# Attention scored in eighths of a unit: own and relative scores mixed on TensorE's row groups, with a block of sums behind each eighth

## The reference

```
q, k, v = conv1x1(wq, xn), conv1x1(wk, xn), conv1x1(wv, xn)     # n, head, c, i, j
qk  = einsum('nhcij,nhciw->nhijw', q, k) / D                    # own scores, a 128 x 128 matrix for each row i
qrq = einsum('nhcij,chjw->nhijw', q, rq) / D                    # relative scores, for each column j
krk = einsum('nhcij,chjw->nhijw', k, rk) / D
weight = softmax(qk + Gq * qrq + Gk * krk, axis=3)              # over j
out = einsum('nhijw,nhciw->nhcij', weight, Gv1 * v)             # v sums, for each i
    + einsum('nhijw,chjw->nhcij', weight, Gv2 * rv)             # r sums, for each j
x = x + conv1x1(wo, out)
```

## Time and profile before

| | us |
|---|---|
| median of 3 runs | 8287.58 |
| lowest and highest | 8284.58, 8298.17 |
| the profiled execution | 8291.75 |
| span of its trace | 8290.0 |
| TensorE busy | 7187.2 (87%) |
| VectorE busy | 5176.6 (62%) |
| ScalarE busy | 4856.3 (59%) |
| GpSimd busy | 2457.0 (30%) |

### The profile page before, as it was taken

One profiled execution on the slowest core, in us unless ns is written; L12 is line 12 of the kernel. 1 busy time (PEld: TensorE's weight loads), 2 busy tenths in 40 slices (PEclk: granted clock), 3 DMA queues, 4 the chain that ended last, 5 costly groups with the idle time before them and its releaser, 6 DMA issues. The chain is left out here.

```text
span 8290.0 us, 275612 instructions
## 1 busy us (share of the span) xinstructions
PE 7187.2 (87%) x106442; PEld 6044.4 (73%) x106442; DVE 5176.6 (62%) x20646; ACT 4856.3 (59%) x11427; POOL 2457.0 (30%) x1235
## 2 busy tenths in 40 slices
PE   4999999799999999999999899999999966766738
PEld 3555555689988888898899898898888932332338
DVE  5444444366666666666666666666666768988830
ACT  1444444577777777777777777777777733333410
POOL 0000000243443443444434444434434432322210
PEclk7999999666666666666666666666667688988855
DMA  7555555565655665655556656656656576766522
GB/s 217 203 203 204 204 204 197 113 112 100 112 103 98 113 107 101 107 99 107 101 106 112 102 100 109 109 99 110 105 100 109 92 232 203 265 201 202 208 74 99
DMA packets 1721071, 1148.11 MB, mean 138 GB/s; under 512 B 1143009, under 2 KB 1506145, under 8 KB 1703329
## 3 DMA queue, kind: packets, MB, share of 16 engines
q1 hardware_dynamic: 1530336, 842.56, 48.1%
q10 hardware_dynamic: 188352, 285.27, 9.3%
q0 software_dynamic: 1024, 2.09, 0.1%
HBM read 708.04 MB, written 421.56 MB: 136 GB/s over the span
## 5 line engine op out<-in xcount | busy, mean ns | idle before, releaser
L787 POOL TENSOR_TENSOR att_scores<-att_scores,att_inverse 128x1024 f32<-128x1024 f32 x1024 | 1966.8, 1934 | 2951.7 <-DVE att_inverse L722 2951.7
L660 ACT ACTIVATE att_scores<-att_scores,att_negmax 128x128 f32<-128x128 f32 x8192 | 2509.2, 399 | 67.6 <-issue 67.6
L737 DVE CUSTOM_DVE_ANT_0 att_scores<-att_ps,att_scores 128x128 f32<-128x128 f32 x8192 | 1780.8, 286 | 1066.7 <-PE att_ps L573 957.5
L560 PE MATMUL att_ps<-att_qk,att_rs 32*128 32x64 f32 x32768 | 1793.2, 380 | 155.6 <-ACT att_scores L652 114.2
L560 PEld LDWEIGHTS att_ps<-att_qk,att_rs 32*128 32x128 f32 x32768 | 1698.6, 299 | 196.2 <-ACT att_scores L652 142.5
L573 PE MATMUL att_ps<-att_own 16*128 16x128 f32 x16384 | 1541.6, 405 | 231.3 <-issue 224.1
L573 PEld LDWEIGHTS att_ps<-att_own 16*128 16x128 f32 x16384 | 1416.2, 300 | 268.9 <-issue 264.4
L652 ACT ACTIVATE att_scores<-att_ps 128x1024 f32<-128x1024 f32 x1024 | 992.4, 1021 | 1044.3 <-PE att_ps L560 1044.3
L720 DVE TENSOR_REDUCE att_total<-att_scores 128x8 f32<-128x1024 f32 x1024 | 1233.7, 1205 | 70.7 <-issue 70.7
L594 PE MATMUL att_ps<-att_scores,att_rv 128*16 128x64 f32 x32768 | 1249.6, 334 | 11.0 <-issue 10.8
L594 PEld LDWEIGHTS att_ps<-att_scores,att_rv 128*16 128x16 f32 x32768 | 1193.6, 127 | 24.5 <-issue 13.1
(11 more groups left out here) (146 smaller groups left out, 5276.0 us busy)
## 6 DMA issues: line engine op xcount, KB each, us to landing
qk<-proj_qk_out ACTq DMA_DIRECT2D x64, 2048.0 KB, 8.5
att_qk<-qk SPq DMA_DIRECT2D x512, 256.0 KB, 6.7
att_own<-qk SPq DMA_DIRECT2D x2048, 64.0 KB, 2.5
proj_x<-in_x_dram SPq DMA_DIRECT2D x128, 512.0 KB, 4.3
v_t<-proj_v_out ACTq DMA_DIRECT2D x64, 1024.0 KB, 11.3
att_vt<-v_t SPq DMA_DIRECT2D x128, 512.0 KB, 5.5
att_v<-att_att_v SPq DMA_DIRECT2D x512, 128.0 KB, 4.2
att_r<-att_att_r SPq DMA_DIRECT2D x512, 128.0 KB, 3.5
```

The source lines that it names most:

```text
L560: last = pe.matmul(ps[:, 4 + g, jj * IU:(jj + 1) * IU], rs[32 * g:32 * g + 32, t * JB + jj, :], qk[b][32 * g:32 * g + 32, :, t * JB + jj], ...
L660: last = act.activation(scores[v][:, i, :], scores[v][:, i, :], ACT.Exp, bias=negmax[v][:, i:i + 1], scale=-1.0)
L737: last = dve.tensor_tensor_reduce(out=scores[v][:, i, :], in0=ps[:, 2 * (p % 2) + r // 4, (r % 4) * W:(r % 4 + 1) * W], in1=scores[v][:, i ...
L787: pool.tensor_tensor(scores[v][:, rows, :], scores[v][:, rows, :], inverse[v][:, rows].unsqueeze(2).broadcast_to([P, PR, W]), ALU.mult).th ...
```

## The change

Own and relative scores are computed together, in eighths of a unit. `ROUNDS` goes from 4 to 8: a relative round now uses two row groups, 2 * (1 - t % 2) and the next, and banks 4 and 5. `scores_of` issues own piece p of unit u on two row groups, and between its matmuls those of a relative round on the other two: round p+2 of unit u+1 for p under 6, round p-6 of unit u+2 for p of 6 and 7. Own operands are 32 rows, of which the upper 16 are zeroed once (`cleared`). After each eighth PE does half of a v fill in bank 6 (8 matmuls) and half of an r fill in bank 7 (16 matmuls): fills 2 and 3 of unit u-2 in the first four eighths, fills 0 and 1 of unit u-1 in the others.

ACT reads a relative round with one instruction, issues exps with a counter per four rows, and reads an r fill behind every second eighth. DVE reads all four v fills and sums rows two pieces behind. `att_v`, `att_r` and `vt` are two halves each; att_r is stored in DRAM in 8 pieces (`STORES_R`), the combine phase reads them so. SP issues the stores of unit u-2 in two parts (16 DMAs a unit in place of 8), the v values in two, `rv` in four; the qk load stands ahead of the first stores. POOL's two scalings of the relative tables stand ahead of pieces 3 and 7 of the seventh unit, before ahead of 2 and 4. Two calls of `unit` stand behind the last unit in place of one.

```diff
-ROUNDS = JG // JB
+ROUNDS = 2 * JG // JB
+HR = PR // 2
+HALVES = IU // HR
-JT = JG
+JT = JG // 2
+STORES_G = JG // JT
...
             def unit(h, k, u, started, left):
                 if started >= 1:
                     sp.wait_ge(own_done, PIECES * u)
                     load_own(h, k, 1)
-                if started >= 2:
-                    store(*before(h, k, 2), u - 2)
-                if started >= 1:
-                    ph, pk = before(h, k, 1)
-                    later(sp, v_done, FILLS * (u - 1))
-                    load_v(ph, pk)
-                    if pk == 0:
-                        later(sp, r_done, FILLS * (u - 1))
-                        load_rv(ph)
                 if left >= 2:
                     sp.wait_ge(rel_done, ROUNDS * u + ROUNDS)
                     load_qk(*after(h, k, 2))
+                if started >= 2:
+                    store(*before(h, k, 2), u - 2, 0)
+                if started >= 1:
+                    ph, pk = before(h, k, 1)
+                    later(sp, v_done, FILLS * (u - 2) + FILLS // 2)
+                    load_v(ph, pk, 0)
...
                 if left >= 1:
                     sp.wait_ge(own_done, PIECES * u + PIECES // 2)
                     load_own(*after(h, k, 1), 0)
+                if started >= 1:
+                    later(sp, v_done, FILLS * (u - 1))
+                    load_v(ph, pk, 1)
...
+                if started >= 2:
+                    store(*before(h, k, 2), u - 2, 1)
...
+            def relative(u, v, t, jj, gg):
+                g, j = 2 * (1 - t % 2) + gg, t // 2 * JB + jj
+                return pe.matmul(ps[:, 4 + gg, jj * IU:(jj + 1) * IU], rs[32 * g:32 * g + 32, j, :], qk[v % 2][32 * g:32 * g + 32, :, j],
+                                 start=True, stop=True, tile_position=(32 * g, 0))
+            def own_score(u, p, r, gg):
+                half, g, at = p // (PIECES // 2), 2 * (p % 2) + gg, p % (PIECES // 2) // 2 * 4 + r
+                return pe.matmul(ps[:, g, r * W:(r + 1) * W], own[half][32 * g:32 * g + 32, 1, at, :], own[half][32 * g:32 * g + 32, 0, at, :],
+                                 start=True, stop=True, tile_position=(32 * g, 0))
+            def scores_of(u, p, now, ru, rv_, t, rel_on):
...
                 for r in range(4):
                     for gg in range(2):
+                        if now:
+                            last_own = own_score(u, p, r, gg)
+                        if rel_on:
+                            for x in range(2):
+                                last_rel = relative(ru, rv_, t, 2 * r + gg, x)
...
+            def unit(u, v, parts):
+                back2, back1, now, ahead1, ahead2 = parts
+                for p in range(PIECES):
+                    if p < 6:
+                        scores_of(u, p, now, u + 1, v + 1, p + 2, ahead1)
                     else:
+                        scores_of(u, p, now, u + 2, v + 2, p - 6, ahead2)
+                    if p < 4 and back2:
+                        sums_with_v(u - 2, v - 2, 2 + p // 2, p % 2)
+                        sums_with_r(u - 2, v - 2, 2 + p // 2, p % 2)
+                    if p >= 4 and back1:
+                        sums_with_v(u - 1, v - 1, p // 2 - 2, p % 2)
+                        sums_with_r(u - 1, v - 1, p // 2 - 2, p % 2)
...
+            def read_relative(u, o, t):
+                pair = 2 * (1 - t % 2)
...
+                act.activation(scores[o % BUFS][:, :, :].rearrange("w i (g j) -> w i g j", g=G)[:, :, pair:pair + 2, t // 2 * JB:(t // 2 + 1) * JB],
+                               ps[:, 4:6, :].rearrange("w g (j i) -> w i g j", i=IU), ACT.Copy).then_inc(rel_read, 1)
...
+            def unit(u, v, parts):
+                for p in range(PIECES):
+                    if p == 0:
+                        if back1:
+                            exp_half(u - 1, v - 1, HALVES - 2)
+                            exp_half(u - 1, v - 1, HALVES - 1)
+                    elif now:
+                        exp_half(u, v, 2 * p - 2)
+                        exp_half(u, v, 2 * p - 1)
+                    if p < 6 and ahead1:
+                        read_relative(u + 1, v + 1, p + 2)
+                    if p >= 6 and ahead2:
+                        read_relative(u + 2, v + 2, p - 6)
+                    if p % 2 and p < 4 and back2:
+                        read_r(u - 2, 2 + p // 2)
+                    if p % 2 and p >= 4 and back1:
+                        read_r(u - 1, p // 2 - 2)
...
-                        if k == UPH - 2 and not last and p in (2, 4):
-                            scale_relative(h + 1, p // 2 - 1)
+                        if k == UPH - 2 and not last and p == 3:
+                            scale_relative(h + 1, 0)
+                        if k == UPH - 2 and not last and p == 7:
+                            scale_relative(h + 1, 1)
```

More of the change, by code:

```diff
@@ L529, in _ @@
                 load_qk(0, k)
+            sp.wait_ge(cleared, 2)
             for half in range(2):
@@ L556, in relative @@
                 if t % (ROUNDS // 2) == 0:
                     pe.wait_ge(rs_ready[t // (ROUNDS // 2)], u // UPH + 1)
[L558 to L565 removed]
+                later(pe, rel_read, ROUNDS * u + t)
@@ L593, in sums_with_r @@
+            def sums_with_r(u, v, b, half):
+                if half == 0:
+                    pe.wait_ge(rv_loaded[b], (u // UPH) * 16 + 16)
+                    later(pe, r_read, FILLS * u + b)
+                for jj in range(half * JB // 2, (half + 1) * JB // 2):
                     for g in range(G):
-                        last = pe.matmul(ps[32 * g:32 * g + HD, bank, jj * IU:(jj + 1) * IU], rv[:, g * JG + b * JB + jj, :], scores[v][:, :, g * JG + b * JB + jj],
+                        j = g * JG + b * JB + jj
+                        last = pe.matmul(ps[32 * g:32 * g + HD, 7, jj * IU:(jj + 1) * IU], rv[:, j, :], scores[v % BUFS][:, :, j],
@@ L640, in _ @@
+            pe.wait_ge(cleared, 3)
             for t in range(ROUNDS):
-                relative(0, 0, t)
+                scores_of(0, 0, False, 0, 0, t, True)
+            for t in range(2):
+                scores_of(0, 0, False, 1, 1, t, True)
             units(pe, unit)
@@ new lines, in read_relative, with exp_half @@
+                act.activation(scores[o % BUFS][:, :, :].rearrange("w i (g j) -> w i g j", g=G)[:, :, pair:pair + 2, t // 2 * JB:(t // 2 + 1) * JB],
+                               ps[:, 4:6, :].rearrange("w g (j i) -> w i g j", i=IU), ACT.Copy).then_inc(rel_read, 1)
+            def exp_half(u, v, p):
+                act.wait_ge(added, HALVES * u + p + 1)
+                for r in range(HR):
+                    i = p * HR + r
+                    last = act.activation(scores[v % BUFS][:, i, :], scores[v % BUFS][:, i, :], ACT.Exp, bias=negmax[v % BUFS][:, i:i + 1], scale=-1.0)
+                last.then_inc(exped, 1)
@@ L710, in _ @@
             for t in range(ROUNDS):
                 read_relative(0, 0, t)
+            for t in range(2):
+                read_relative(1, 1, t)
             units(act, unit)
@@ L741, in unit @@
[L741 to L771 removed]
+                    if r % HR == HR - 1:
+                        last.then_inc(added, 1)
@@ new lines, in _, with unit @@
+            BEHIND = 2
+            def unit(u, v, parts):
+                back2, back1, now, ahead1, ahead2 = parts
+                for p in range(PIECES):
+                    if now:
+                        add_and_largest(u, v, p)
+                    if p % 2 == 1 and p < 4 and back2:
+                        read_v(u - 2, 2 + p // 2)
+                    if p % 2 == 1 and p >= 4 and back1:
+                        read_v(u - 1, p // 2 - 2)
+                    k = p - BEHIND
+                    if k >= 0 and now:
+                        sums_of(u, v, k)
+                    elif k < 0 and back1:
+                        sums_of(u - 1, (v - 1) % BUFS, PIECES + k)
@@ L773, in _ @@
+            for half in range(2):
+                dve.memset(own[half][:, :, :, :], 0.0).then_inc(cleared, 1)
+            dve.memset(ps[:, 6:8, :], 0.0).then_inc(cleared, 1)
             units(dve, unit)
```

286 lines of the change are left out of this document (88 added, 198 removed).

## The result

The changed kernel takes 7861.41 us (7833.53 to 7865.77, four runs), the kernel before 8286.08 in the same comparison: a ratio of 0.9478, with a 95% interval of 0.9454 to 0.9502. Its profiled execution took 7833.53 us, with a span of 7831.8.

A forecast was written before the change was run, and what follows sets the result against it. Attention was taken as bound by TensorE, mostly at half clock. Unit 32.6 + 3.75 + 2.1 = 38.45 against 40.05 us, times 124, -198; prologue +36, combine +5: 8291.75 becomes 8135 profiled, 8130 forecast, range 7880 to 8900.

The forecast's parts named there:

- blocks of 2 us would not win the clock back: Attention, after a pause: short sums may regain full clock late; 1.2 units per head taken at half clock.
- An eighth on PE alone: PE in attention: scores, v sums, r sums and turns of one eighth take 3.81 us at full clock.
- The tables: Next head's relative tables, loaded by SP and scaled by POOL: PE waits 12 us per head where it waited 4.
- The prologue: Before attention: four relative rounds of 5.75 us become ten of about 4.8, +27 us.
- Combine: Combine stage, bound by DVE: r sums are read in pieces half as long, +5 us, bounds 0 and 20.
- The loop's pauses: PE at and just behind the turn of the loop over four units: pauses stay, 18 us per head.
- ACT's chain: ACT's exps, relative reads and r read: a pair of eighths takes 8.15 us, an undisturbed unit 32.6.
- The v values: SP's loads for the v sums: named among those queued behind a late store, with no separate price.
- The rival that rested on this queue: SP's issues fill the unit: 9 to 12 us more per head, 8270 to 8320 us, chance 0.12.
- The clock's price: Attention: 1.2 units per head at half clock, 13.8 us each, add 2.1 us per unit.
- the "better" case: Row groups overlap more, or rounds ahead cover pauses: unit 35 to 36.9 us, total 7700 to 7940, chance 0.10.
- The turn between tile modes: PE between sums and scores: 0.2 us a turn, 2 turns a unit become 16, +2.8 us.

The follow-up runs named there:

- the block experiments: Changed kernel with a unit's sums gathered into one, two or four blocks in place of eight: 9711.82, 9612.95 and 8935.01 us.
- p_pad40: Kernel before, with 40 already met waits on PE ahead of its first relative round, shifting its later instructions: 8160.04 us, 0.9852 of before.
- c_act_order: Changed kernel, but ACT reads the relative round between the two halves of an eighth's exps, not behind both: 7779.01 us, 0.9398 of the kernel before.
- e_vt_first: Changed kernel, but SP issues the first half of the v values at the head of a unit, ahead of own, qk and stores: 7704.9 us.
- a_unmixed: Changed kernel, but each eighth issues the own piece first and the relative round behind it, unmixed: 7984.86 us, 0.9651 of the kernel before.
- b4_blocks: Changed kernel, but a whole v fill and r fill behind every second eighth, four blocks of sums a unit: 8935.01 us, 1.0785 of the kernel before.
- b_block: Changed kernel, but all sums of a unit in one block behind its eighth eighth: 9711.82 us, 1.1737 of the kernel before.

## Why the prediction was wrong, step by step

**What held.** Attention was bound by TensorE and by its clock: the clock went from 0.68 to 0.93, where 0.92 was forecast, and the block experiments show that the place of the sums did it. The worry that blocks of 2 us would not win the clock back was priced at 1.2 of a head's eight units at half clock; it was 14% of the time. An eighth on PE alone was put at 3.81 us and takes 3.70: scores with the turn behind them 1.98 for 1.99, v sums 0.45 for 0.50, r sums with their turn 1.27 for 1.32. The tables were to cost 12 us a head and cost 168.3 / 14 = 12.0. The prologue was to cost 27 us more up to the first own piece and cost 28.5 (1575.0 against 1546.5), though its terms, ten rounds of 4.8 for four of 5.75, make 25. Combine was to cost 5 more and cost nothing.

**The loop's pauses "stay, 18 us per head".** This step failed, and it was one of the two largest errors. They came to 89.7 us in 4000, 6.5 per head. 11.5 us a head are 1.4 a unit, some 180 us. A part was a wrong reading: the earlier trace rows gives 196.7 / 12.5 = 15.8 us a head, and of its five pauses a head one stands away from the turn; the other 2.2 us of the 18 were never pauses ahead of an own piece. p_pad40 shows what two thirds of it are: the kernel before, with its loop shifted, gives back 126 us. The pause away from the turn, up to 4 us once a head (3.85 at 3417.40), which the trace puts down to issue, is gone too; by its place it was an own load queued behind the tables, which is argued and not shown. The step took a number of the profile for a property of the loop, when two pauses 7 records apart at one turn were the sign that the place of the code had a part in it.

**ACT's chain, 8.15 us a pair.** It is 7.77. The laying out in time was right in its order, and c_act_order shows that this order is what makes PE wait. But it added lengths of rows, where the prediction's own rule for PE was to take distances of starts. Eight exps are 2.35 us from start to the next start (3046.94 to 3049.29) and not 2.44, a relative read 0.91 and not 1.0, an r read 0.5 and not 0.58. Laid out again with these, the prediction's chain ends at 7.76: exp to 2.35, relative to 3.26, fill done at 4.0, r read to 4.5, exp to 6.85, relative to 7.76. So the undisturbed unit was 31.1 and not 32.6: 1.5 us, 185 in all.

**The v values.** The prediction named them as queued behind a late store and gave them no price: 1.4 us a unit, the one error in the other direction, 175 us. It had SP's queue at 30 to 32 us of 32.6, "without slack"; with a unit of 31 this was over the edge. The trace agrees with its count: SP waits 498 us of 4000 in the changed kernel, 4.5 of a unit's 36.04, so its issues fill 31.5. e_vt_first shows that the place in this queue was the cause. The rival that rested on this queue had the right mechanism, but its size was offset by the two errors above.

**The clock's price.** 2.1 us a unit were reckoned; what is left over in the measured unit is 36.04 - 31.1 - 4.0 (all pauses) = 0.9. A part is in the reckoning: 1.2 units of 46.4 us a head are 18% of the time, and 14% was measured. A part is that the half clock also falls on pauses, where nothing runs that it could slow: between 3000 and 4000 us the clock is at 0.50 for 140 us, and in 20 of them PE does nothing. By the prediction's own price, 13.8 us in 46.4, these two leave about 1.3. The 0.9 is a remainder and not measured, and the 0.4 between them stays open.

In sum: 38.45 less 1.5 (ACT's chain), less 1.4 (the loop), plus 1.4 (v values), less 1.2 (the clock's price) and plus 0.3 of smaller waits make the 36.04 measured. 2.4 us a unit times 124 are 298 us, and 8135 lies 301.5 above the profiled 7833.53. The range's lower end had only the "better" case for this and cut it at 7880; the case itself, 7700 to 7940 with chance 0.10, is where the time fell, but by luck: the reasons that it gave, a faster mix and a lead that covers the pauses, are not the ones that the runs show.

**What the change itself is worth.** Beside the kernel before with a loop that lies well (8160.04) the changed kernel gains 3.7%, not 5.2%. Taking the mixing out costs 123 us (a_unmixed), gathering the sums costs 1074 or more (b4_blocks); the two don't add up to the gain, as each stands on the other: the distributed sums cover the read that a round on two banks needs.

**The turn between tile modes.** The last seven relative records of an eighth begin at 3020.29. Four of them take some 0.22 us earlier in that eighth, 0.056 each, so they would be through at 3020.68, and the v sums start at 3020.84: 0.15 us for the turn, an estimate from starts. If the other end costs as much, 16 turns are 2.4 us a unit, a little less than reckoned. The Trainium skill, page "TensorEngine Tiling (Array Packing)", section Key Properties, says that a change of mode drains the engine; the trace agrees as far as it shows a gap there, and with half the turns, in b4_blocks, the kernel was 1074 us slower.

## What to carry to other kernels

Where the clock is what a stage lacks, spread the work that raises it over the stage in pieces no further apart than the trace shows the clock to last, and check at the same time what each piece covers: here it covered the read of a single-buffered PSUM pair as well. When every engine's chain is laid out in time, take distances between starts for all of them. Before a loop's pauses are carried over into a forecast, look at how many there are per turn and where they stand, for their number can belong to the place of the code and not to the change; and when waits for different loads rise and fall against each other as issues are reordered, the loads share a queue that has no slack for them, and moving a part of it to another engine is worth trying (here 124 us).

## What the runs showed of the hardware

- A second pause at a loop's turn on PE, 2.7 to 3.9 us long at the turns read in the kernel before, 7 records behind the first. It moved to 1 record behind with 24 instructions ahead of the loop, and vanished with 40 (63, 61 and 35 pauses in 4000 us).
- The granted clock fell while scores ran without sums: 3.4 us behind the last sums with PE busy throughout (before, 3496.94), 5.2 in the earlier trace rows, 4.0 in b_block, 5.7 in b4_blocks. It stayed at 0.50 in busy scores, and was back about 2 to 5 us after sums began (before: 3071.50 to 3073.7 and 3034.20 to 3039.5; the changed kernel: 3082.97 to 3086), even where a block of sums is only 2 us long.
- Own matmuls of 16 and of 32 rows on a row group made no difference to the time (7857.03 and 7861.41 us) or to the clock (0.92 and 0.93 over 4000 us).
- Relative records on two row groups take 1.98 us to the next sums by themselves (a_unmixed) and with own records mixed in on the other two (3018.86 to 3020.84).
